# One convolution tap moved from ScalarE to GpSimd in a two-layer adaLN block with a Mamba scan

## The reference

```python
def _causal_conv1d(u, w, b):
    ut = jnp.pad(jnp.transpose(u, (0, 2, 1)), ((0, 0), (0, 0), (D_CONV - 1, 0)))
    y = jax.lax.conv_general_dilated(ut, w[:, None, :], window_strides=(1,), padding='VALID',
                                     feature_group_count=D_INNER, ...)
    return jnp.transpose(y + b[None, :, None], (0, 2, 1))
...
xz = jnp.einsum('bld,ed->ble', x, W_in)
u, z = jnp.split(xz, 2, axis=-1)
u = _silu(_causal_conv1d(u, conv_w, conv_b))
x_dbl = jnp.einsum('bld,rd->blr', u, W_x)
dt, Bm, Cm = jnp.split(x_dbl, [DT_RANK, DT_RANK + D_STATE], axis=-1)
dt = jax.nn.softplus(jnp.einsum('blr,dr->bld', dt, W_dt) + b_dt)
y = _selective_scan(u, dt, A, Bm, Cm, Dvec)
y = y * _silu(z)
return jnp.einsum('bld,od->blo', y, W_out)
```

## Time and profile before

| what | value |
|---|---|
| median of three executions | 747.61 us (744.85 to 749.23) |
| the profiled execution's own time | 745.24 us |
| its span in the profile | 743.3 us |
| mean granted clock of TensorE | 0.907 of full |
| busy in the span: TensorE, VectorE, ScalarE, GpSimd | 84%, 79%, 67%, 62% |
| the chain of waits that ended last, from 452.50 us on, share of the span | TensorE 26%, VectorE 5%, GpSimd 3%, ScalarE 1% |
| L751, the last tap, 16 instructions on ScalarE | 662 to 702 ns each |

### The profile page before, as it was taken

How to read it: one execution, slowest core, us unless ns; L and a number is a source line. 1 busy time by engine, 2 the same in 40 slices (tenths; PEclk the granted TensorE clock), 3 DMA queues, 4 the chain that set the end, 5 groups by cost and what they waited for, 6 DMA issues and landing times. The chain is left out here.

```text
span 743.3 us, 8867 instructions
## 1 busy us (share of the span) xinstructions
PE 626.3 (84%) x2909; PEld 390.4 (53%) x2909; DVE 584.5 (79%) x818; ACT 496.7 (67%) x935; POOL 459.7 (62%) x261
## 2 busy tenths in 40 slices
PE   3955777886899999999997899999999970799991
PEld 2343455523555555656432555555655560699881
DVE  6794998675999999999666899999999849654421
ACT  3643534688999898889478999898988562123330
POOL 0136665101798989889401598989888424378866
PEclk9876899897899999999998899999999955699996
DMA  5000000002232323333002123233323171023323
GB/s 202 0 3 1 1 1 0 1 4 75 60 98 83 108 91 100 97 89 99 15 4 69 63 90 94 94 98 92 100 88 98 52 288 56 9 30 34 40 30 28
DMA packets 30780, 48.05 MB, mean 65 GB/s; under 512 B 3736, under 2 KB 12328, under 8 KB 30224
## 3 DMA queue, kind: packets, MB, share of 16 engines
q1 hardware_dynamic: 25600, 44.45, 18.7%
q0 software_dynamic: 5136, 3.05, 3.8%
HBM read 42.98 MB, written 4.49 MB: 64 GB/s over the span
## 5 line engine op out<-in xcount | busy, mean ns | idle before, releaser
L481 POOL TENSOR_TENSOR hc_all<-hs_all,c_row 128x1024 f32<-128x1024 f32 x87 | 204.7, 2367 | 107.6 <-DVE hs_all L1680 107.1
L1159 PE MATMUL ps<-hc_all,ident 128*128 128x512 f32 x508 | 236.9, 598 | 2.6 <-POOL hc_all L481 2.6
L1680 DVE TENSOR_TENSOR_SCAN hs_all<-da,ps 128x1024 f32<-128x1024 f32 x88 | 197.7, 2270 | 13.7 <-ACT da L815 9.1
L815 ACT ACTIVATE da<-big,a_neg 128x511 f32<-128x511 f32 x256 | 169.3, 709 | 30.5 <-DVE w_ffn L1680 28.9
L1159 PEld LDWEIGHTS ps<-hc_all,ident 128*128 128x128 f32 x508 | 90.2, 192 | 86.8 <-issue 76.9
L481 POOL TENSOR_TENSOR hc_all<-w_ffn,c_row 128x1024 f32<-128x1024 f32 x40 | 94.6, 2365 | 29.8 <-DVE w_ffn L1680 26.4
L1680 DVE TENSOR_TENSOR_SCAN w_ffn<-da,ps 128x1024 f32<-128x1024 f32 x40 | 91.4, 2285 | 4.2 <-ACT da L815 0.9
L1179 PE MATMUL ps<-ident,dbu 128*128 128x128 f32 x464 | 61.2, 276 | 10.7 <-ACT dbu L790 5.5
L1179 PEld LDWEIGHTS ps<-ident,dbu 128*128 128x128 f32 x464 | 53.5, 142 | 25.3 <-issue 18.1
L551 POOL DMA_INDIRECT out<-hc_all,hs_all x32 | 54.0, 1689 | 12.0 <-issue 7.3
L892 ACT ACTIVATE big<-ps,b 128x516 f32<-128x516 f32 x32 | 22.1, 690 | 47.1 <-PE ps L1350 47.1
(11 more groups left out here) (308 smaller groups left out, 1017.5 us busy)
## 6 DMA issues: line engine op xcount, KB each, us to landing
c_row<-c_rows SPq DMA_DIRECT2D x128, 256.0 KB, 3.1
tmpA<-w_in SPq DMA_DIRECT2D x2, 1024.0 KB, 7.0
tmpB<-w_in SPq DMA_DIRECT2D x2, 1024.0 KB, 9.4
x_tok<-x_in SPq DMA_DIRECT2D x2, 512.0 KB, 5.8
out<-x_tok SPq DMA_DIRECT2D x1, 1024.0 KB, 11.9
xm_rows<-xn SPq DMA_DIRECT2D x1, 1024.0 KB, 5.1
w_mod<-w_mod_in SPq DMA_DIRECT2D x2, 384.0 KB, 6.6
w_ffn<-w_ffn_in SPq DMA_DIRECT2D x1, 560.0 KB, 7.9
```

The lines of the kernel that those rows point to most:

```text
L481: nc.gpsimd.tensor_tensor(hc[:, n % 4, :, :], hs3[HS_BUF[n]].rearrange("p (i s) -> p i s", i=IC), c_row[:, n % 4, :].unsqueeze(1).to_broad ...
L815: ins = nc.scalar.activation(da[:, n % 2, i, 1:S], dtT[:, b, i, 1:S], ACT.Exp, scale=a_neg[:, l, i, n:n + 1])
L1159: mm = nc.tensor.matmul(ps[:, YS + i, :], ident[:], hc[:, n % 4, i, :], start=(n == 0), stop=(n == NS - 1))
L1680: v.tensor_tensor_scan(hs3[HS_BUF[n]], decay, pair.rearrange("p i s -> p (i s)"), 0.0, ALU.mult, ALU.add).then_inc(c_scan, 1)
```

## The change

GpSimd makes the last tap, from `u_pad` in SBUF (it takes the view that starts at column `KC - 1`, which holds the same numbers as the bank). ScalarE's two instructions a batch are gone. GpSimd's 8 instructions of a layer stand ahead of its scan, which for layer 1 is behind both memsets. `m_u0` is now counted up once a batch, by the copy alone, and VectorE waits for a new semaphore, `m_tap`. To have a semaphore free, the load of `bt_rows` counts on `ld_ffn`, so that those who waited for `w_ffn` now wait for both loads.

```diff
-            sp.dma_start(bt_rows[:], bt_in).then_inc(ld_bt, 16)
+            sp.dma_start(bt_rows[:], bt_in).then_inc(ld_ffn, 16)
...
-            pool.wait_ge(ld_bt, 16)
+            pool.wait_ge(ld_ffn, 32)
...
             for l in range(L):
                 q = sems[l]
+
+                for b in range(B):
+                    pool.wait_ge(q["m_u0"], b + 1)
+                    after(pool, q["m_u"], IC * (b - 1))
+                    for i in range(IC):
+                        ins = nc.gpsimd.tensor_scalar(conv[:, b % 2, i, :], u_pad[:, b % 2, i, KC - 1:SP],
+                                                      vec(V_CW + (l * IC + i) * KC + KC - 1), None, ALU.mult)
+                    ins.then_inc(m_tap, 1)
...
                         nc.scalar.copy(u_pad[:, b % 2, :, KC - 1:SP], ps[:, u_bank:u_bank + IC, :]).then_inc(q["m_u0"], 1)
-                        after(act, q["m_u"], IC * (b - 1))
-                        for i in range(IC):
-                            ins = nc.scalar.activation(conv[:, b % 2, i, :], ps[:, u_bank + i, :], ACT.Identity,
-                                                       scale=vec(V_CW + (l * IC + i) * KC + KC - 1))
-                        ins.then_inc(q["m_u0"], 1)
...
-                        pe.wait_ge(q["m_u0"], 2 * b)
+                        pe.wait_ge(q["m_u0"], b)
                 elif l or b > 1:
-                    after(pe, q[["m_u0", "m_z"][half]], [2, 1][half] * b)
+                    after(pe, q[["m_u0", "m_z"][half]], b)
...
-            dve.wait_ge(ld_ffn, 16)
+            dve.wait_ge(ld_ffn, 32)
...
-                        dve.wait_ge(q["m_u0"], 2 * b + 2)
+                        dve.wait_ge(m_tap, B * l + b + 1)
```

More of the change, by code:

```diff
@@ L284, in chunk_at @@
             return HC * e + c + (1 if e == E - 1 else 0)
-        ld_vec, ld_attn, ld_bt = sem("ld_vec"), sem("ld_attn"), sem("ld_bt")
+        ld_vec, ld_attn, m_tap = sem("ld_vec"), sem("ld_attn"), sem("m_tap")
         ld_x, ld_mod = [sem(f"ld_x_{k}") for k in range(2)], [sem(f"ld_mod_{l}") for l in range(2)]
```

## The result

Both kernels were timed side by side on one chip. The changed kernel took **760.39 us** (median of four, 757.45 to 762.96), the kernel before 748.42 there: ratio **1.0155 [1.0113, 1.0197]**, slower by 1.1 to 2.0%. The forecast was 755.2, the range 749.5 to 762.0. The profiled execution took 757.45 (span 755.7, mean clock 0.892) against 745.24 (743.3, 0.907) before. Executions over 1.5% above the fastest of their kernel are left out of every ratio here.

A forecast was written before the change was run, and what follows sets the result against it. Bound: in the two preludes, the last hand-over between engines, none busy throughout. Layer 0 +0.9, layer 1 +7.0 and TensorE's clock +2.1 made +10.0 us on the profiled 745.24: 755.2 us, range 749.5 to 762.

The forecast's parts named there:

- rival 3: GpSimd's tap takes 1.4 us, the rate of two inputs: 4.8 us more, 760.0 us in all; chance 0.14.
- The merged loads, 0 us: At the start, the wait for both loads on one semaphore is over before VectorE first asks for `w_ffn`: 0.
- The tap, 1.0 us: In both preludes, one GpSimd tap of 512 elements takes 1.0 us; a pair takes 2.0 where ScalarE's took 1.27.
- Layer 0, +0.9: Prelude of layer 0: GpSimd's second pair delays VectorE's six instructions, so L1141 starts 0.9 us later; -1.2 without exclusion.
- The batches behind add nothing: Prelude of layer 0, batches 2 and 3: slack and waits for TensorE cover GpSimd's slower pairs, adding 0.
- Layer 1, +7.0: Prelude of layer 1: first taps blocked behind the second memset and slower, 4.9 us, plus 2.1 of exclusion.
- The exclusion, each in turn for a whole instruction: In both preludes, VectorE's two-input instructions and GpSimd's SBUF-reading taps block each other for whole instructions: 2.1 us per overlap.
- rival 1: In both preludes, the exclusion between GpSimd and VectorE costs nothing: +5.8 us, 751.0 us in all; chance 0.30.
- The clock, +2.1: Prelude of layer 1: TensorE idles 7.7 us, then works at half clock, losing 2.1 us; least 0.
- The later batches of layer 1: Prelude of layer 1, batches behind the first two: they cover their taps as in layer 0, adding nothing.
- Each further 0.1 us of tap adds up to 1.2 us: Six GpSimd instructions per layer count one after the other, so each further 0.1 us of tap adds up to 1.2.
- Rival 4, ScalarE the bound: ScalarE bounds the preludes, so taking its pairs off gains time: -3.2 us, 742.0 us in all; chance 0.06.

The follow-up runs named there:

- the kernel that only writes: The changed kernel with GpSimd filling the tap's columns and a spare tile with constants, reading nothing from SBUF, instead of making the tap: 760.58 us, ratio 1.0193.
- the 766.13 us execution: Profiled execution, in a second set, of the changed kernel with ScalarE's taps kept in layer 0: 766.13 us; that set's ratio to the kernel before 1.0140.

## Why the prediction held

The forecast (slower, 755.2) was right in sign, in where most of the loss lies and in how it comes about there, and the result is in its range. The size was in part luck. The sum had 10.0 us; the preludes grew by 14.66, which is rival 3's 14.8 (a slower tap), and the untouched stretches gave back 2.3 that nothing explains. Two errors cancel inside layer 1 besides.

- *The merged loads, 0 us.* Right as far as can be seen: the stretch up to the zero-fill is not longer, and ScalarE's tap with the same semaphores gave 1.0024.
- *The tap, 1.0 us.* **This is the term that was mis-sized.** It halved the slope of two-input operations for one input. Measured: 1.56 us. Between 0.60 at 128 elements and 1.56 at 512 lie 2.5 ns for each element, more than the 2.1 of two inputs, so rival 3's 1.4 was not even the end. The row that spoke for it (L462 slower than L443 at equal size) stood in the earlier trace rows, and I gave it a chance of 0.14. The Trainium skill's "roughly line-rate" for one input ("GPSIMD Engine Reference", section "Engine selection"), from which 0.91 us had been estimated, is not borne out by any tap here.
- *Layer 0, +0.9.* The first w_x came at +0.01 from the zero-fill. VectorE began 1.79 later (pair 3.1 us), which takes back what the freed bank and the nearly missing exclusion gave. "The batches behind add nothing" was wrong: in the last batch a pair of 3.1 us exceeds the 1.76 us of cover by 1.3, and VectorE began 28.43 us behind the zero-fill in place of 26.95. In the profiled execution that delay is hidden behind the slow matmuls, through which all of the +2.57 came in; where the clock held it moved the last w_x by 0.83. The sum had no clock in layer 0.
- *Layer 1, +7.0.* Measured 6.88 up to `y_sb`. The 4.2 of the blocked queue and the place of the first tap were right; the slower pair cost 1.85 in place of 0.75, and the exclusion 0.85 in place of 2.1. One row's too little met the other's too much.
- *The exclusion, each in turn for a whole instruction.* Too strong for this operation. VectorE's instructions beside GpSimd's took 1.09 to 1.17 us where 0.75 is alone, and GpSimd's lost 1.17, 0.21 and 0.47 us in layer 0 and 0.22 in layer 1. So the rule named in the prediction ("SBUF — State Buffer", section "Who interferes with whom" of the Trainium skill) is not met by the one-input tap as a whole instruction. That section says of a VectorE instruction with two SBUF inputs that it contends with a GpSimd instruction that reads SBUF, and calls contention an exclusive lock; "for the whole instruction" it says of VectorE's two-port modes, and the prediction carried it over. The two-input tap comes close to such a rule, with single taps of VectorE at 1.52 and of GpSimd at 1.49 (alone 0.75 and 1.04). On this term rival 1, which had the exclusion free, is nearer the truth for the changed kernel than the forecast was.
- *The clock, +2.1.* Right in kind and place: idle for 7.76 us, 0.50 behind it, 2.93 us by experiment. The sum read its own rows too low: from the return at 46.42 until past 51.0 or 52 are 4.6 to 5.6 us at half clock, not 3.5 to 5.3, and half of that is 2.3 to 2.8. Missed were 1.33 us at the last w_x of layer 1 (with the clock up there, in the kernel with GpSimd in layer 1 only, that part took 3.87 again), and layer 0.
- *The later batches of layer 1.* They were to cover their taps. The last w_x was 1.03 later, its SiLU waiting 1.30 us for VectorE's taps: the pair too long for its cover, as in layer 0.
- *Each further 0.1 us of tap adds up to 1.2 us.* From 1.56 to 0.92 us layer 1 gave back 4.62, which is 0.72 for each 0.1 and a bit over the 0.6 of one layer, but 1.33 of the 4.62 is the clock that stayed up at the last w_x; by two inputs it gave only 0.3, as the exclusion grew.
- *Rival 4, ScalarE the bound:* out. Its waits for TensorE ahead of the `dt` rows in layer 0 grew from 3.4 to 5.2 us in three.

Open is why the clock falls in layer 0. With GpSimd's tap there it fell between 160 and 172 us in nine of ten profiles (in the tenth, the kernel that only writes, at 172.2), without it in one of four, that of the 766.13 us execution; filling the wait of 1.9 us ahead of the first w_x did not stop it. That the change makes the fall likelier is what these counts suggest and do not show.

## What to carry to other kernels

Before moving work to a free engine, read the queue it joins: what the instructions ahead of it wait for counts more than their own time (4.83 us here for two taps behind one memset). A price per element must come from a row of the same operation and form, and a row of it at another size is a warning, not a detail, when it is slower than its neighbour. An idle stretch made on TensorE can be paid twice, once as the wait and once as the slow clock behind it (7.76 us idle and 2.93 more here). And where the clock falls from one execution to the next in a stretch of full work, read a gain of 2 us in that stretch from more than one profile.

## What the runs showed of the hardware

- GpSimd's TENSOR_SCALAR with a weight per partition took 0.60, 0.92 and 1.56 us for 128, 256 and 512 f32 elements a partition; a TENSOR_TENSOR with the weight broadcast took 1.04 us for 512. The one-input form is the slower one.
- What GpSimd takes from VectorE depends on what GpSimd does. Beside 3.1 us of memsets, VectorE's six lost nothing; beside one-input products 0.85 us; beside two-input ones 1.6 us in less time. The faster product cost the neighbour more.
- In layer 1 TensorE's clock fell to 0.50 in idle stretches of 7.76 and 6.01 us and within half a microsecond of its return from one of 2.93, and stayed at 1.00 right behind 1.84 and 1.66. A long idle stretch isn't needed: it also fell at 393.8 us with 0.67 us idle in the 18 us before, and in layer 0 at 162.6 us, 13.8 us behind a stretch of 1.92, while before the change it stayed up through that prelude behind 2.42 us.
